# A routed expert layer after sparse attention on one core: idle products on an operand of VectorE, new instruction orders, gates as weights in four column groups, input scale and offset on VectorE, last additions in another order

## The reference

```python
# x: 4 x 512 x 512, ctx: 4 x 512 x 128 (4 batches of 512 tokens)
def adjacency(h, adj_raw, Wq, Wk, gamma_raw):
    sim = einsum('bhnd,bhmd->bnm', Q, K) / (sqrt(d) * H)      # 512 x 512 for each batch
    k = int(512 * 0.3)
    mask = sim >= kth_largest(sim, k)                         # per row
    A = sigmoid(sim) * mask
    A = (A + A.T) * 0.5
    return (1 - gamma) * adj_raw + gamma * A

def experts(x, ...):                                          # 8 experts, the best 2 for each token
    probs = softmax(x @ gate_w)
    combine = normalised best two, times alpha
    h = gelu(x @ fc1_w[e] + fc1_b[e])                         # 512 -> 512
    y = h @ fc2_w[e] + fc2_b[e]                               # 512 -> 512
    return sum over e of combine[:, e] * y[e]

x = x + tanh(g_xattn) * adjacency(ctx, layernorm(x), ...)
x = x + tanh(g_ffn) * experts(layernorm(x), ...)
```

## Time and profile before

| | us |
|---|---|
| runs (3) | 365.43, 366.69, 367.62; median 366.69 |
| profiled execution | 365.13 |
| its span | 363.4 |
| TensorE busy | 324.3 (89%) |
| VectorE busy | 200.7 (55%) |
| ScalarE busy | 165.0 (45%) |
| GpSimd busy | 100.1 (28%) |

### The profile page before, as it was taken

How to read it: one execution, slowest core, us unless ns; L and a number is a source line. 1 busy time by engine, 2 the same in 40 slices (tenths; PEclk the granted TensorE clock), 3 DMA queues, 4 the chain that set the end, 5 groups by cost and what they waited for, 6 DMA issues and landing times.

```text
span 363.4 us, 6131 instructions
## 1 busy us (share of the span) xinstructions
PE 324.3 (89%) x1937; PEld 232.9 (64%) x1937; DVE 200.7 (55%) x697; ACT 165.0 (45%) x384; POOL 100.1 (28%) x141
## 2 busy tenths in 40 slices
PE   6906899779998999899999989999999999999960
PEld 4402667677764786678778576777785877577610
DVE  0488698887879777898886372636206112311010
ACT  2485515389996746256786222232222213132320
POOL 5001001361111357114307431331733111312031
PEclk9975699899999999999999999999999999999996
DMA  2999989977974696876627587744678854533253
GB/s 91 379 392 369 352 298 331 378 267 139 305 145 123 144 243 231 146 161 183 113 54 181 191 173 135 211 100 81 203 163 149 176 119 104 111 64 87 30 74 46
DMA packets 53636, 65.79 MB, mean 181 GB/s; under 512 B 9792, under 2 KB 28512, under 8 KB 53600
## 3 DMA queue, kind: packets, MB, share of 16 engines
q1 hardware_dynamic: 46144, 47.99, 43.7%
q0 software_dynamic: 7456, 17.37, 24.7%
HBM read 39.56 MB, written 25.78 MB: 180 GB/s over the span
## 4 chain that ended last, share of the span: by engine, by line
PE 50%; issue 18%; DVE 14%; DVEq 5%; DMA 5%; POOL 3%; POOLq 2%; ACT 2%; ACTq 0%
PE ps L1711 21%; PE ps L1684 13%; PE ps L1694 10%; DMA out_rows<-ab,dst 3%; PE ps L1647 2%; POOL xs_rows L566 2%; DMA meta<-xs_rows 2%; DVE top L1087 1%; DVE stats L1012 1%; PE ps L1607 1%; PE ps L1721 1%; PE ps L1627 1%; PE ps L1639 1%; POOLq L530 1%; DVEq L1086 1%
## 5 line engine op out<-in xcount | busy, mean ns | idle before, releaser
L1684 PEld LDWEIGHTS ps<-xgT_r,weights 128*128 128x128 f32 x768 | 87.8, 192 | 8.3 <-issue 6.7
L1684 PE MATMUL ps<-xgT_r,weights 128*128 128x128 f32 x768 | 89.6, 276 | 3.6 <-ACT xgT_r L743 2.0
L1711 PE MATMUL ps<-weights,act_r 128*128 128x512 f32 x192 | 86.3, 595 | 1.5 <-ACT act_r L766 1.5
L580 POOL DMA_INDIRECT out_rows<-ys,dst x24 | 37.9, 1578 | 115.2 <-ACT ys L773 70.0
L1711 PEld LDWEIGHTS ps<-weights,act_r 128*128 128x128 f32 x192 | 34.9, 190 | 38.4 <-issue 36.5
L766 ACT ACTIVATE act_r<-ps,b1T 128x128 f32<-128x128 f32 x96 | 27.1, 365 | 38.9 <-PE ps L1684 38.8
L1694 PEld LDWEIGHTS ps<-sim,weights 128*128 128x128 f32 x256 | 35.2, 190 | 1.9 <-issue 1.7
L566 POOL DMA_INDIRECT xs_rows<-ab,pos x32 | 31.9, 998 | 14.5 <-issue 9.1
L1694 PE MATMUL ps<-sim,weights 128*128 128x160 f32 x256 | 35.6, 299 | 0.0
L773 ACT ACTIVATE ys<-ys,meta 128x512 f32<-128x512 f32 x24 | 17.3, 719 | 31.3 <-DVE ys L1322 31.3
L1322 DVE TENSOR_TENSOR ys<-ps,b_r 128x512 f32<-128x512 f32 x24 | 16.5, 686 | 23.4 <-PE ps L1711 22.0
(11 more groups left out here) (206 smaller groups left out, 419.0 us busy)
## 6 DMA issues: line engine op xcount, KB each, us to landing
weights<-in_L_ffn_fc_w SPq DMA_DIRECT2D x16, 1024.0 KB, 8.0
b_r<-in_L_ffn_fc_b SPq DMA_DIRECT2D x32, 256.0 KB, 4.1
xg_r<-xs_rows SPq DMA_DIRECT2D x88, 64.0 KB
xb<-in_x SPq DMA_DIRECT2D x4, 1024.0 KB, 7.1
out_rows<-xb SPq DMA_DIRECT2D x4, 1024.0 KB, 5.5
sim<-xs_rows SPq DMA_DIRECT2D x32, 80.0 KB
xs_rows<-weights SPq DMA_DIRECT2D x1, 2064.0 KB, 13.5
xs_rows<-weights SPq DMA_DIRECT2D x2, 516.0 KB, 5.9
```

Source lines behind the costliest of these rows:

```text
L580: pool.indirect_dma_start(out=out_rows, out_offset=bass.IndirectOffsetOnAxis(ap=dst[:, k % 2, e:e + 1], axis=0), in_=result_rows(m), in_of ...
L1684: mm = pe.matmul(ps[:, n % 2, i * P:(i + 1) * P], weights[:, e, 0, h, i * P:(i + 1) * P], rows[:, h * P:(h + 1) * P], start=(h == 0), stop ...
L1711: mm = pe.matmul(ps[:, 2 + m % 2, :], rows, weights[:, e, 1, i, :], start=(i == 0), stop=(i == IB - 1))
```

## The change

1. The idle products of TensorE take a new operand `warm`, written by VectorE, instead of `ones_b` of GpSimd; the first group grows from 24 to 36, and groups of 8 are put ahead of the first projection, ahead of the first scores and elsewhere.
2. The instruction orders of all five engines are written anew.
3. The input's scale and offset, a pass of ScalarE (`affine_x`), go into the two VectorE instructions `total` and `add`, which become three-operand instructions.
4. For batches 1 to 3 (the second to the fourth), the gate matrix is the weights (`gate_by_token`): four products, each with 32 columns of weights (8 used, the rest zero), into four column groups of one bank, over 128 tokens; ScalarE copies the result (`logits_out`), and one product with `by_block` (`gate_by_row`) sums the four groups and gives rows by token. Batch 0 keeps `gate`.
5. The last result, of batch 3, expert 7, is numbered behind the second tails. Rows which it shares with those tails are handed over to it on TensorE (`hand_over`); it is then free to be added while the tails' addition is in flight. Its `layer2` is cut in two halves around `hand_over` and `merge(1)`, and its bias and weighing are two VectorE instructions (`open_last`, `close_last`).

```diff
-BUSY_LOADS, BUSY_SEARCH, BUSY_MASK = 24, 36, 48
+BUSY_LOADS, BUSY_SEARCH, BUSY_MASK = 36, 36, 48
...
         def result_no(k, e):
-            return k * E + e if k < BATCH - 1 else FULL + (SHARE + 1) * (e // SHARE) + e % SHARE
+            if k < BATCH - 1:
+                return k * E + e
+            return LAST_NO if e == E - 1 else FULL + (SHARE + 1) * (e // SHARE) + e % SHARE
...
# GpSimd, add_result
+                if m == LAST_NO:
+                    pool.wait_ge(twins_ok, 1)
+                    pool.wait_ge(last_ok, 1)
+                    pool.wait_ge(added, 16 * (m - 1))
...
# ScalarE
-            def affine_x(b, t):
-                i = b * BT + t
-                act.wait_ge(xa_ok, b + 1)
-                act.activation(xb[:, b % 2, t, :], xb[:, b % 2, t, :], ACT.Identity, scale=xa_scale[:, i:i + 1],
-                               bias=xa_bias[:, i:i + 1]).then_inc(xa_done, 1)
+            def logits_out(b, t):
+                n = BT * (b - 1) + t
+                act.wait_ge(logT_done, n + 1)
+                if n >= 2:
+                    act.wait_ge(gate_ps, BT + n - 1)
+                act.copy(logT[:, t % 2, :], logT_ps).then_inc(logT_sb, 1)
...
# VectorE, total and add
-                dve.wait_ge(xa_done, i + 1)
-                dve.tensor_tensor(xb[:, b % 2, t, :], xb[:, b % 2, t, :], ab[:, b % 2, t, 0:SEQ], ALU.add)
+                dve.scalar_tensor_tensor(xb[:, b % 2, t, :], xb[:, b % 2, t, :], xa_scale[:, i:i + 1], ab[:, b % 2, t, 0:SEQ],
+                                         ALU.mult, ALU.add)
...
-                dve.tensor_tensor(xb[:, b % 2, t, :], xb[:, b % 2, t, :], ps[:, SIDE_BANK + t % 2, :],
-                                  ALU.add).then_inc(x1_sb, 1)
+                dve.scalar_tensor_tensor(xb[:, b % 2, t, :], xb[:, b % 2, t, :], xa_bias[:, i:i + 1],
+                                         ps[:, SIDE_BANK + t % 2, :], ALU.add, ALU.add).then_inc(x1_sb, 1)
...
+            def open_last():
+                u = LAST_NO % 2
+                dve.wait_ge(handed_ps, 1)
+                dve.wait_ge(b2_in_s[u], b2_count(LAST_NO))
+                dve.wait_ge(added, freed(LAST_NO))
+                dve.scalar_tensor_tensor(result_rows(LAST_NO), b2_r[:, u, :], last_share, ps[:, SMALL_BANK, :], ALU.mult,
+                                         ALU.add)
+            def close_last():
+                u = LAST_NO % 2
+                dve.drain()
+                dve.wait_ge(y_ps, LAST_NO + 1)
+                dve.scalar_tensor_tensor(result_rows(LAST_NO), ps[:, 2 + u, :], last_share, result_rows(LAST_NO), ALU.mult,
+                                         ALU.add).then_inc(last_ok, 1)
...
+            dve.memset(warm[:], 1.0).then_inc(warm_ok, 1)
+            dve.wait_ge(consts, 2)
+            for k in range(KB):
+                part = slice(k * QUAD, (k + 1) * QUAD)
+                dve.tensor_copy(by_block[part, :], ident[part, k * QUAD:k * QUAD + E])
             coefficients()
...
# TensorE
             def keep_busy(matmuls):
                 with pe.Fori(0, matmuls // 4):
                     for _ in range(4):
-                        pe.matmul(ps[:, 3, 0:P], ones_b[:], ones_b[:], start=True, stop=True)
+                        pe.matmul(ps[:, 3, 0:P], warm[:], warm[:], start=True, stop=True)
...
+            def gate_by_token(b, t):
+                n = BT * (b - 1) + t
+                pe.wait_ge(x1T_sb, BT + n + 1)
+                if t == 0 and b < BATCH - 1:
+                    pe.wait_ge(q_sb, b + 2)
+                if n:
+                    pe.wait_ge(logT_sb, n)
+                for k in range(KB):
+                    mm = pe.matmul(logT_ps[k * QUAD:(k + 1) * QUAD, :], gate_w[:, k, :],
+                                   x1T[:, t % 2, k * P:(k + 1) * P], start=True, stop=True)
+                mm.then_inc(logT_done, 1)
+
+            def gate_by_row(b, t):
+                pe.wait_ge(logT_sb, BT * (b - 1) + t + 1)
+                pe.matmul(logit_ps[:, t, :], logT[:, t % 2, :], by_block[:], start=True, stop=True).then_inc(gate_ps, 1)
...
+            def hand_over():
+                pe.wait_ge(tails_w, GROUPS)
+                pe.wait_ge(twins_ok, 1)
+                pe.matmul(ps[:, SMALL_BANK, :], twins[:, GROUPS, :], result_rows(tail_no_of(GROUPS - 1)), start=True,
+                          stop=True).then_inc(handed_ps, 1)
...
-            pe.wait_ge(consts, 2)
-            keep_busy(BUSY_LOADS)
+            pe.wait_ge(warm_ok, 1)
+            keep_busy(BUSY_LOADS)
+            pe.wait_ge(consts, 2)
             pe.wait_ge(qk_in, 32)
             pe.matmul(ps[:, 0, 0:C], wq, wk, start=True, stop=True).then_inc(m_ps, 1)
             turn_context(0)
             pe.wait_ge(m_sb, 1)
+            keep_busy(8)
             project(0)
+            keep_busy(8)
...
             layer2(3, 6)
-            layer2(3, 7)
             tails(1)
+            layer2(3, 7, 0, 2)
+            hand_over()
             merge(1)
+            layer2(3, 7, 2, 4)
```

716 lines of the change are left out of this document (394 added, 322 removed).

## The result

The changed kernel takes 375.85 us (median of 3 runs, 375.15 to 376.32) against 366.69 before: a ratio of 1.0251, 95% interval 1.0195 to 1.0306. It is slower by 2.5%, where 1.5% faster was forecast; the time lies outside the range. Timed once more on another chip the ratio was 1.0221 (1.0181 to 1.0261).

The account below looks back on a forecast made before the run. Limits differ by part: front, body of nearly gapless TensorE (VectorE up to `rank(1)`), and a tail of chained additions. 340.9 + 17.1 = 358.0 span, 359.7 with 1.7 around it, plus 1.6 to the median: 361.3 us; range 355.0 to 367.5.

Parts of the forecast that it names:

- The start: TensorE's first products: idle products begin near 9.6 us, `m_qk` at 13.4; the clock returns part, front shift +5.5 us.
- the other case that I had named, idle products near 1 us: At the start of TensorE: if idle products begin near 1, then 8 us better.
- The front: Up to the first expert product: steps of −7.8 us and the +5.5 shift put it at 76.3 instead of 78.56.
- The body up to `rank(1)`: From the first expert product: VectorE sets the pace, its stretch 55.3 us; `rank(1)` at 127.9, before 129.66.
- From `rank(1)` to the end of `layer2(3,6)`: 213.0 us instead of 213.8: scores +2.6, gates −1.2, two gaps −2.4, transposition +0.2; end at 340.9.
- one of my own signs of being wrong: In the body: rows of (2,0) or (3,0) stopping TensorE would show the forecast wrong.
- rival (C): Rows of batch 2 come late, with a GpSimd addition between scatters; 9 us late gives 369.5; chance 0.10.
- The gates: Gates of batches 2 to 4 on TensorE: 0.64 us each, −0.15 each; bounds 0.32 and 1.28.
- The tail: After L, the end of `layer2(3,6)`: two additions in flight, end at L + 17.1 instead of L + 19.9, −2.8 us.
- Scale and offset on VectorE: Three-operand instructions cost 0.06 us more each, 1.9 for 32; with PSUM at most 0.1 each; ScalarE's gain is slack.
- The rivals: Three other cases: 356.4 us (chance 0.20), no change at 366.6 (0.15), slower through late rows of batch 2 (0.10).

Follow-up runs that it names:

- a_warm: Changed kernel with VectorE writing the idle products' operand `warm` ahead of its wait for the constants; ratio 1.0052 to the kernel before.
- a_sync: Changed kernel with the bias of (0,2) loaded ahead of the rows of (0,4) and expert 7's weights loaded earlier; ratio 1.0093 to the kernel before.
- a_again: The changed kernel as it is, timed again on another chip; ratio 1.0221 to the kernel before.
- a_scale: Changed kernel with GpSimd's `xn_scale` of the fourth batch ahead of the addition of (1,7); ratio 1.0196 to the kernel before.
- m_rows: a_mend with GpSimd's addition of (2,4) behind all eight scatters of batch 3 instead of behind six; ratio 0.9796 to the kernel before.
- a_mend: The mended kernel: the changed kernel with the edits of a_sync, a_scale and a_warm together; ratio 0.9787 to the kernel before.
- a_fill: Changed kernel with the filling of `xs_rows` one place earlier on SyncE, ahead of the rows of (0,4); ratio 1.0180 to the kernel before.
- a_w7: Changed kernel with only expert 7's 2 MB of weights loaded earlier, behind the load of x for the third batch; ratio 1.0263 to the kernel before.
- a_place: Changed kernel with VectorE asking for the bias of (0,2) behind the masks of batch 1, load order kept; ratio 1.0261 to the kernel before.
- m_serial: a_mend with the last addition waiting until the tails' addition has landed; ratio 0.9888 to the kernel before.
- a_bias: Changed kernel with only the bias of (0,2) loaded earlier, ahead of the rows of (0,4); 370.18 us, ratio 1.0159 to the kernel before.

## Why the prediction was wrong

**The start: right.** I said that `warm` stands behind the wait for all constants: first idle product forecast at 9.6, measured 9.84; `m_qk` 13.4 and 13.66; score pieces at full clock, as said. The first guess on VectorE comes at 23.98 instead of 18.78: +5.2, where I had put +5.5. a_warm prices the other case that I had named, idle products near 1 us: 6 to 7 us of the run, where I had written 8.

**The front: right.** 76.3 forecast, 76.88 measured. One step of it isn't in my sum: the steps as written put `one_hot(1)` 2.3 later than before, not the 4.0 that I gave; measured are 4.2 (72.73).

**The body up to `rank(1)`: this is the step that failed.** I set `member` of batch 1 between 127.1 and 128.5, by adding up VectorE's own instructions and the waits of the trace before, and counted only what the new order took out ahead of it. Two lines of that order put `add_bias(2)` and `add_bias(3)` ahead of the masks and of the sums, and each needs a bias row from SyncE, whose queue I had not followed beyond the row loads. VectorE's stretch from the end of `one_hot(1)` to the end of `member` took 64.4 us (72.73 to 137.18) where I had 55.3: 9.1 more, which is the wait of 9.08. In total the rest of that sum came out. `rank(1)` came 9.4 late, 0.6 of it from the front. In a_sync, where both loads are in time, `rank(1)` is 5.7 earlier than in a_again; of what is left, 2.1 us is the scatter that the early weights delay.

**From `rank(1)` to the end of `layer2(3,6)`: the second step that failed.** 213.0 forecast, 220.0 measured. Six score pieces behind `rank(1)` took 4.96 instead of 2.6 (+2.4), the drain behind the addition cost a stop of 1.84 and 1.8 at the low clock (shown by a_scale), the rows of (3,0) 1.06, one of my own signs of being wrong (m_rows takes such a wait away). These make 7.1. The slow score pieces are not the late bias's doing: they take 5.29 in a_sync (granted clock 0.51) and 4.85 in a_mend (0.57), where no bias is waited for. I had forecast that TensorE would stand ahead of `rank(1)` and had put the pieces behind it at full clock all the same. In a_fill, a_w7 and a_place they do run at full clock, and why there and not elsewhere stays open. I had written of GpSimd's new order only in rival (C), and looked there for scatters behind additions, not for `xn_scale` behind one. The trace before had the price: with an addition at 115.47, `xn_scale` of batch 1 stood 3.54 us between its halves.

**The gates: right.** 0.64 forecast. Measured are 0.35 for the four products, 0.09 on the line ahead of them and 0.14 for the product by rows, 0.58 together; with 0.21 to 0.25 for a product by rows beside a gate it is up to 0.69. Four products at once were put at 0.22, so by the rows a change of form costs the 0.09 ahead and at most 0.13 in the gate itself, against my 0.08 + 0.14 from `tails`, and up to 0.11 more where a product by rows follows at once. By the drain on a change of tiling mode in the Trainium skill, TensorEngine Tiling (Array Packing), Tiling Modes, an entry into another form drains TensorE; the trace agrees in direction, with 0.09 us to at most 0.33 us for entry and exit together.

**The tail: right.** L + 17.1 forecast, L + 17.3 measured, and step by step: the last two additions start at L + 8.6 and L + 10.5, forecast at 8.2 and 10.1; m_serial shows that the second addition in flight is worth 3.5 of it.

**Scale and offset on VectorE: right.** Four three-operand `total` took 2.74, as forecast by four `mask`, and two `add` with PSUM as third operand 1.41, where two plain `add` took 1.28 before (at 112.24): 0.06 each for `total`, and 0.07 for `add`. The second is within the bound of 0.1.

**The rivals.** None was the case. (C) named the right side and even a bias 9 us late, at a price of 369.5; but it had the bias of (1,4), queued behind the places of batch 2, and dismissed it, and rows of (2,0) that stop TensorE, which they did not. The range ended at 367.5, below that price, and no case had a bias of batch 0 late.

The mended kernel, at 0.9787, is near the forecast for the change, 0.985 (361.3 to 366.69), but that is in part luck. The forecast has the late `warm` in it, and the mended kernel has not. Less the 6 to 7 us that a_warm gives, the forecast would be 0.966 to 0.969, below the mended kernel's interval.

## What to carry to other kernels

When an order is written anew, follow for every wait of the engine that sets the pace where the thing waited for now stands in its own queue, the small loads above all: here a 256 KB bias row behind 3 MB of filling, which had landed 10.9 us ahead of its reader, came 9.1 us behind it in the new orders, and stopped whatever was queued behind that reader. Put large transfers that nobody awaits where neither small loads nor scatters are in flight, and a computation with a drain ahead of an indirect transfer, not behind it. After mending one late load look for the next, since a single mend here gained a part (a_bias) or nothing (a_place, a_w7).
